# A second buffer for the first layer's products, and the remainder's rows loaded one half pair earlier

## What is computed

```python
def _cin_layer(h, h0, W, b):
    Wr = W.reshape(W.shape[0], Hn, Mn)
    x = jnp.einsum('bhd,bmd,ohm->bod', h, h0, Wr) + b[None, :, None]
    return jax.nn.relu(x)

x1 = _cin_layer(e, e, W1, b1)            # 128 outputs from 32 x 32 products
direct2 = _cin_layer(x1[:, :64], e, W2, b2)   # 128 outputs from 64 x 32 products
z = sum over d of [x1[:, 64:], direct2]
```

## Time and profile before

| | |
|---|---|
| profiled execution | 2057.63 us |
| its span, first to last instruction | 2055.8 us |
| mean granted TensorE clock | 0.996 |
| TensorE (PE) busy | 2012.2 us, 98% |
| VectorE (DVE) busy | 1983.9 us, 96% |
| ScalarE (ACT) busy | 1631.9 us, 79% |
| GpSimd (POOL) busy | 1524.0 us, 74% |

### The profile page before, as it was taken

How to read it: one execution, slowest core, us unless ns; L and a number is a source line. 1 busy time by engine, 2 the same in 40 slices (tenths; PEclk the granted TensorE clock), 3 DMA queues, 4 the chain that set the end, 5 groups by cost and what they waited for, 6 DMA issues and landing times.

```text
span 2055.8 us, 28705 instructions
## 1 busy us (share of the span) xinstructions
PE 2012.2 (98%) x6890; PEld 1299.2 (63%) x6890; DVE 1983.9 (96%) x545; ACT 1631.9 (79%) x4755; POOL 1524.0 (74%) x580
## 2 busy tenths in 40 slices
PE   3899999999999999999999999999999999999999
PEld 1566666666666666666666666666666666666664
DVE  5999999999999999999999999999999999999992
ACT  2788788788888888887887887887887888888873
POOL 3877787787787787787787788778778777778520
PEclk9999999999999999999999999999999999999999
DMA  6777777776776776776776776776777777767740
GB/s 185 215 210 208 198 213 203 198 217 199 200 214 200 204 215 196 207 216 190 211 213 195 208 216 192 210 212 191 215 208 197 211 205 201 212 200 206 210 108 1
DMA packets 239331, 406.51 MB, mean 198 GB/s; under 512 B 33377, under 2 KB 50273, under 8 KB 239090
## 3 DMA queue, kind: packets, MB, share of 16 engines
q1 hardware_dynamic: 231026, 397.10, 66.7%
q0 software_dynamic: 8192, 8.40, 2.0%
HBM read 321.49 MB, written 16.78 MB: 165 GB/s over the span
## 4 chain that ended last, share of the span: by engine, by line
DVE 59%; issue 35%; PE 3%; DMA 1%; SPq 1%; ACT 0%; DVEq 0%; POOL 0%; ACTq 0%; POOLq 0%
DVE pnear L459 27%; DVE pfar L459 16%; DVE plo L464 16%; PE acc L521 0%; ACT phi L655 0%; PE acc L527 0%; PE acc L538 0%; PE x1p L586 0%; PE acc L586 0%; PE acc L528 0%; DMA near<-emb_rows 0%; POOL gathered L237 0%; DMA rem_b<-emb_rows 0%; SPq L301 0%; PE acc L592 0%
## 5 line engine op out<-in xcount | busy, mean ns | idle before, releaser
L237 POOL DMA_INDIRECT gathered<-in_tables,idx x256 | 762.0, 2977 | 104.8 <-issue 52.8
L258 POOL TENSOR_TENSOR prod<-near,h 128x2048 f32<-128x2048 f32 x126 | 577.2, 4581 | 174.4 <-PE acc L522 168.7
L655 ACT CAST phi<-pnear 128x4096 fp32r<-128x4096 f32 x128 | 465.9, 3640 | 269.9 <-DVE pnear L459 269.9
L527 PE MATMUL acc<-phi,w2lo 128*128 128x512 f32 x1536 | 603.9, 393 | 14.3 <-ACT phi L655 14.3
L528 PE MATMUL acc<-phi,w2hi 128*128 128x512 f32 x1536 | 603.1, 393 | 0.0
L602 ACT ACTIVATE acc<-acc,bias 128x64 f32<-128x64 f32 (+1 forms) x2048 | 574.9, 283 | 11.7 <-PE acc L528 8.5
L464 DVE TENSOR_TENSOR plo<-pnear,phi 128x4096 fp32r<-128x4096 f32 x128 | 571.8, 4467 | 2.0 <-ACT phi L655 2.0
L459 DVE TENSOR_TENSOR pfar<-far,x1p 128x4096 f32<-128x4096 f32 x128 | 565.8, 4420 | 6.9 <-PE acc L538 1.1
L459 DVE TENSOR_TENSOR pnear<-near,x1p 128x4096 f32<-128x4096 f32 x128 | 564.9, 4414 | 4.7 <-ACT x1p L638 4.7
L521 PE MATMUL acc<-prod,w1T 128*128 128x512 f32 x1024 | 462.5, 594 | 14.3 <-DVE prod L444 12.9
L538 PE MATMUL acc<-pfar,w2T 128*128 128x512 f32 x1024 | 460.3, 592 | 0.0
(11 more groups left out here) (68 smaller groups left out, 535.5 us busy)
## 6 DMA issues: line engine op xcount, KB each, us to landing
near<-emb_rows SPq DMA_DIRECT2D x512, 256.0 KB
far<-emb_rows SPq DMA_DIRECT2D x512, 256.0 KB, 4.2
x1rep<-x SPq DMA_DIRECT2D x256, 256.0 KB, 4.2
h<-emb_rows SPq DMA_DIRECT2D x128, 256.0 KB
emb_rows<-gathered SPq DMA_DIRECT2D x128, 128.0 KB, 3.5
gathered<-in_tables,idx POOLq DMA_INDIRECT x256, 4.9
rem_a<-emb_rows SPq DMA_DIRECT2D x64, 64.0 KB, 3.6
rem_b<-emb_rows SPq DMA_DIRECT2D x64, 64.0 KB, 3.0
```

What stands on the lines that cost most here:

```text
L237: nc.gpsimd.indirect_dma_start(out=gathered[s][:, g, :], out_offset=None, in_=a["tables"], in_offset=bass.IndirectOffsetOnAxis(ap=idx[s][: ...
L258: nc.gpsimd.tensor_tensor(prod1[:, :, :], near[(u + 2) % 3][:, :, :], h0[odd][:, :].unsqueeze(1).to_broadcast([P, K1, N]), ALU.mult).then_ ...
L527: nc.tensor.matmul(acc2[s][:, :], w2lo[:, t, :], phi[:, t, :], start=(t == 0), stop=False)
L655: nc.scalar.copy(phi[:, 0:T_NEAR, :], pnear[:, :, :, :].rearrange("p a k n -> p (a k) n")).then_inc(hi_near_ready, 1)
```

## The change

It gives `prod1` two buffers (even and odd chunks), and relaxes the wait of GpSimd by one chunk. VectorE's second `products1` loses its wait for the first `layer1`. On SyncE's list two things move: the store of a gathered pair goes ahead of the `far` loads in the even step, and the remainder's rows are loaded at the end of the even step (after the `far` loads, behind a wait for the store just issued) in place of between `x1rep` and `near` in the odd step.

```diff
-        prod1 = sb("prod1", [P, K1, N])
+        prod1 = [sb(f"prod1_{s}", [P, K1, N]) for s in range(2)]
...
-                    pool.wait_ge(acc1_ready, c + 2)
+                    pool.wait_ge(acc1_ready, c + 1 if begun(at) else 2)
                     pool.wait_ge(near_in[(u + 2) % 3], LOADS * (turn * (U // 3)) + LOADS * ((u + 2) // 3 + 1))
-                    nc.gpsimd.tensor_tensor(prod1[:, :, :], near[(u + 2) % 3][:, :, :],
+                    nc.gpsimd.tensor_tensor(prod1[odd][:, :, :], near[(u + 2) % 3][:, :, :],
...
-                if odd and within(at, 3):
-
-                    sp.wait_ge(emb_stored, STORES * pair + 3 * STORES)
-                    sp.wait_ge(rem_prod_ready, pair + 2)
-                    load_rem((c + 3) * N)
                 if within(at, 3):
 
                     sp.wait_ge(pnear_ready, c + 1)
                     sp.wait_ge(p1_ready, c + 2)
                     load_near((c + 3) * N, 1 - odd, u % 3)
+                if not odd and within(at, 5):
+                    store_rows(pair + 2, (u // 2 + 2) % 3, turn + (u // 2 + 2) // 3 + 1)
                 if within(at, 2):
                     sp.wait_ge(pfar_ready, c + 1)
                     load_far((c + 2) * N, odd)
                 if not odd and within(at, 5):
-                    store_rows(pair + 2, (u // 2 + 2) % 3, turn + (u // 2 + 2) // 3 + 1)
+
+                    sp.wait_ge(emb_stored, STORES * pair + 3 * STORES)
+                    sp.sem_inc(stores_begun, 1)
+                    sp.wait_ge(rem_prod_ready, pair + 2)
+                    load_rem((c + 4) * N)
...
             products1(0)
-            dve.wait_ge(acc1_ready, 1)
             products1(1)
...
                 for k in range(K1):
-                    nc.tensor.matmul(acc1[s][:, :], w1T[:, k, :], prod1[:, k, :], start=(k == 0), stop=False)
+                    nc.tensor.matmul(acc1[s][:, :], w1T[:, k, :], prod1[s][:, k, :], start=(k == 0), stop=False)
```

More of the change, by code:

```diff
@@ L110, in build_dlrm @@
         w2n = far[1][:, :, :].rearrange("o a n -> o (a n)")
-        w1wide = prod1[:, :, :].rearrange("o a n -> o (a n)")
+        w1wide = prod1[0][:, :, :].rearrange("o a n -> o (a n)")
         w2wide = pnear[:, :, :, :].rearrange("o a k n -> o (a k n)")
@@ L115, in build_dlrm @@
         hid1 = [pnear[:, 0, :, :], pnear[:, 1, :, :]]
-        hid2 = [prod1[:, 2 * h:2 * h + 2, :] for h in range(2)]
+        hid2 = [prod1[0][:, 2 * h:2 * h + 2, :] for h in range(2)]
         w1_in = sem("w1_in")
@@ L443, in products1 @@
                 dve.wait_ge(near_in[s], LOADS)
-                nc.vector.tensor_tensor(prod1[:, :, :], near[s][:, :, :],
+                nc.vector.tensor_tensor(prod1[s][:, :, :], near[s][:, :, :],
                                         h0[s][:, :].unsqueeze(1).to_broadcast([P, K1, N]), ALU.mult).then_inc(p1_ready, 1)
```

## The result

The changed kernel takes **2568.88 us** (median of 6 runs, 2566.97 to 2576.03), the kernel before 2057.78 us beside it. The ratio is 1.2496, with a 95% interval from 1.2477 to 1.2515: 25% slower. The forecast was 2573 us.

What follows compares the result with a forecast made beforehand. TensorE was taken to pace at 15.36 us a step, VectorE having only 0.16 us to spare. With collisions, 123 x 19.55 = 2404.7 replaces 1888.7, adding 516 to 2057.6: 2573 us, range 2300 to 2625.

Steps and rivals of the forecast that it cites:

- What paces: TensorE paces at 15.36 us a step, VectorE could do 15.20; an earlier product by itself buys nothing.
- The mechanism: GpSimd and VectorE exclude each other in line 464 (plo near, plo far); whichever comes second stands until the other's instruction ends.
- point 1: `near` lands 11.6 us after `pnear` starts, inside plo near, so a free GpSimd runs `prod` ahead of plo far.
- point 2: GpSimd finishes its gathers at 1026.7, just before plo near at 1026.89, so it is free when `near` lands.
- the chain argument: Once `prod` delays plo far in one step, GpSimd gains room, so each following step collides too.
- point 4: SyncE's moved store and remainder loads make nothing late: 0.
- point 3: `prod` ahead of plo far costs VectorE 4.35 us, making its step 19.55 us, above TensorE's 15.36.
- Point 5: VectorE's lost wait in `products1` gains 0, since TensorE's first `phi` matmul waits 11.5 us for ScalarE.
- point 6: TensorE gets about 4.2 us idle a step and loses 1.7 us to a lower clock; 17.1 stays below 19.55.
- What would show it: Signs in the changed profile: plo far about 6.6 us, steps 19.5 us apart, TensorE some 4 us idle a step.
- One step of a pair: Rival: a gather held inside plo near makes `prod` harmless in every other step; +248, 2306 us; chance 0.09.
- No collision: Rival: `prod` runs behind plo far, beside `pnear`, and costs 0; TensorE still paces, 2057 us; chance 0.10.

Runs made afterwards that it cites:

- the PSUM run: Changed kernel with both subtractions of line 464 reading `x1p` from PSUM in place of `phi` from SBUF (low parts then not right); 2054.10 us, ratio 0.9978.
- one push: Two buffers and lower count with SyncE's old order, plus the two gathers of step 4 issued in step 5; 2563.28 us, ratio 1.2424.
- a good start: Changed kernel with GpSimd waiting for plo far of the step before in steps 1 to 5 alone; 2557.51 us, ratio 1.2427.
- e3_wait_plo_far: Changed kernel with one more GpSimd wait: `prod` of chunk c + 2 waits until plo far of chunk c - 1 is done; 2057.16 us, ratio 0.9994.
- e2_buffers_only: Changed kernel with SyncE's order put back as before, keeping two buffers and the lower count; 2072.79 us, ratio 1.0081.
- e1_old_wait: Changed kernel with GpSimd's old wait for `layer1` of chunk c + 1 put back; 2056.46 us, ratio 0.9991.

## Why the prediction was right

- **What paces.** Right. With `prod` held in place, steps are 15.35 us with the new buffers and SyncE's new order (first run), and where `prod` came early and harmed nothing (the PSUM run) they are 15.35 too: the earlier product bought nothing.
- **The mechanism** was read from two stretches of the trace before: `prod` ahead of plo near, and `rem_parts` behind it. The order of events of the second, GpSimd stands in plo near and then goes ahead of plo far, is what 123 steps show. The PSUM run shows that it hangs on the second operand of line 464.
- **Landing of `near` (point 1).** Estimated at 11.6 us after `pnear` starts; measured 1010.98 - 999.75 = 11.2 in the step shown, and 11.0 to 12.4 over the 123 steps, all inside plo near.
- **Is GpSimd free (point 2).** Right, and the chain argument too: one push starts it, and a good start does not stop it. What the prediction underrated is how narrow the way in was: 0.5 us in step 2, and 0.2 to 0.4 in the odd steps of `e3_wait_plo_far`. It walked in through an odd step; the profiled execution went in through step 2, an even one, by the same cause one step earlier. That it began so soon has some luck in it; that it began at all has little, since in that run every odd step from 3 on offers the way. It saw that the remainder's rows must be early for its walk, and priced SyncE's move itself at 0 (point 4); the move costs nothing where it stands, but without it the chain does not start until the gathers end.
- **Price (point 3).** 4.35 predicted, 4.33 measured (19.53 - 15.20). The sum of 123 x 19.55 had the count of steps right. The rule of the Trainium skill ("SBUF — State Buffer", "SBUF: two separate sides"), that the pair is held for the whole instruction, would have given 4.58 a step, by my estimate some 28 us more than the forecast. By the recorded durations about 0.25 us of an instruction does not block; whether that is the hold or the ends of the record cannot be told here, for GpSimd's rows overlap by a little too (`prod` of step 2 ends on record at 99.42, and the next row starts at 99.38).
- **Point 5** (VectorE's `products1`): no gain, as said; step 0 of the changed kernel starts at 44.62 against 44.66.
- **TensorE's clock (point 6).** 4.2 us a step to fill, with 1.7 of them lost to the clock, was forecast; measured are 4.17, of which 1.4 went to the clock and 2.8 were idle. "What would show it" asked for some 4 us of idle time and so forgot to take the clock's part off. The loss stayed under cover.
- **Rivals.** One step of a pair: `prod` did this in no profiled run. No collision: this is what `e2_buffers_only` does for 121 steps, with a gather as the guard, which the prediction named for the first rival. The gathers missed it by 0.2 to 0.5 us, so it was nearer than a chance of 0.10 suggests.

## What to carry to other kernels

A wait that looks like a cost can be what keeps two engines apart. Before taking one away, ask where on the other engines the freed instruction will now fall. Where VectorE is nearly full and has `tensor_tensor` instructions on two SBUF operands, GpSimd's long instructions belong beside VectorE instructions that read PSUM, and a wait for the end of the last sensitive one is a cheap way to hold them there (ratio 0.9994 here). If they cannot be placed, cut them small: it costs one of them each time, not their sum.

## What was not expected

- The kernel has two steady rhythms, 15.4 and 19.5 us a step, with the same instructions: which one it takes is decided by whether one gather gets out ahead of plo near. In the profiled executions neither rhythm was left while gathers went on.
- A gather is held up as well: started inside plo near it takes as much as 5.3 us in place of 1.0, though VectorE did not stand for it. The Trainium skill ("SBUF — State Buffer", "Who interferes with whom") infers that making descriptors is not held up by `tensor_tensor`; here the gather was, and in its first part: one that starts 0.53 us ahead of plo near (1028.74 against 1029.27 in `e1_old_wait`) takes 0.95 us and ends inside it. Which of its accesses stands, the traces do not show. It happened to protect the kernel with the lower count and SyncE's old order.
- The hold is a little shorter than the instruction's recorded time: 1.3, 2.4 and 4.6 us on record hold VectorE for 1.07, 2.15 and 4.33.
